# Layer 3 of three batch tiles in two column halves, and their layer 4 ahead of the next tile's layer 1

## The reference

```python
fm = emb_table[jnp.arange(N_CAT)[None, :], cat_idx]          # gather, 26 x 128 per sample
h = relu(dense_x @ Wd1 + bd1); h = relu(h @ Wd2 + bd2)
dense = relu(h @ Wdf + bdf)
Z = concatenate([fm, dense[:, None, :]], axis=1)             # 27 x 128
S = einsum('bie,bje->bij', Z, Z)
x = concatenate([S[:, iu, ju], dense], axis=-1)              # 351 + 128
x = relu(x @ Wt1 + bt1)                                      # 1024
x = relu(x @ Wt2 + bt2)                                      # 1024
x = relu(x @ Wt3 + bt3)                                      # 512
x = relu(x @ Wt4 + bt4)                                      # 256
return sigmoid(x @ Wo + bo)
```

## Time and profile before

| | |
|---|---|
| median of 3 runs | 173.36 us (173.22 to 175.69) |
| the profiled execution | 173.28 us, of which the span from first to last instruction is 171.5 us |
| instructions | 3942 |
| PE busy | 160.8 us, 94% of the span |
| PE weight loads | 115.3 us, 67% |
| DVE, ACT, POOL busy | 71.0, 67.0 and 99.2 us |
| granted TensorE clock | 1.000 over the span |

### The profile page before, as it was taken

The page is one execution under the profiler, slowest core; times in us unless marked ns, Lnnn a source line. Parts: engine busy times, 40 slices in busy tenths (PEclk is TensorE's granted clock), DMA queues, the critical chain, the costliest instruction groups (busy, mean ns, idle before and its releaser), DMA issues.

```text
span 171.5 us, 3942 instructions
## 1 busy us (share of the span) xinstructions
PE 160.8 (94%) x1703; PEld 115.3 (67%) x1703; DVE 71.0 (41%) x143; ACT 67.0 (39%) x121; POOL 99.2 (58%) x111
## 2 busy tenths in 40 slices
PE   1999998867799999999999999999999999999995
PEld 1334464423677878767877886777777777788993
DVE  4005267953657457363513045244122262322230
ACT  3368598755657767142202132411111231201202
POOL 3777777777777777777777777777777000000000
DMA  3999655665997552122212222122222000000000
GB/s 49 279 387 310 185 170 177 175 184 168 307 341 259 171 179 55 54 61 46 61 50 57 54 54 57 46 61 50 58 49 57 23 4 0 0 4 0 0 0 0
DMA packets 6674, 18.18 MB, mean 106 GB/s; under 512 B 2309, under 2 KB 2441, under 8 KB 6530
## 3 DMA queue, kind: packets, MB, share of 16 engines
q1 hardware_dynamic: 3330, 11.12, 19.8%
q0 software_dynamic: 3328, 6.82, 15.3%
HBM read 17.93 MB, written 0.00 MB: 105 GB/s over the span
## 4 chain that ended last, share of the span: by engine, by line
PE 71%; DMA 23%; ACT 3%; DVE 1%; issue 0%
PE mp L489 27%; DMA w<-in_wt 22%; PE mp L456 10%; PE mp L514 8%; PE tp L464 6%; PE gp L417 5%; PE gp L407 5%; PE gp L533 3%; PE tp L550 3%; PE gp L429 1%; DMA idx<-in_cat_idx 1%; PE mp L558 1%; ACT xb L671 1%; DVE xb L829 1%; ACT xp L673 1%; ACT w2h L636 1%
## 5 line engine op out<-in xcount | busy, mean ns | idle before, releaser
L350 POOL DMA_INDIRECT rows<-in_emb,row_of x104 | 98.3, 945 | 33.3 <-issue 29.6
L489 PE MATMUL mp<-w2l,a1h 128*128 128x512 f32 x64 | 26.8, 418 | 0.0
L489 PE MATMUL mp<-w2h,a1h 128*128 128x512 f32 x64 | 26.1, 408 | 0.0
L489 PE MATMUL mp<-w2h,a1l 128*128 128x512 f32 x64 | 25.4, 397 | 0.0
L407 PE MATMUL gp<-ident,rows 128*128 128x128 f32 x104 | 17.3, 276 | 2.6 <-DMA rows<-in_emb,row_of 2.5
L662 ACT COPY zt<-gp 128x512 f32<-128x512 f32 x16 | 9.4, 586 | 25.3 <-PE gp L407 25.1
L407 PEld LDWEIGHTS gp<-ident,rows 128*128 128x128 f32 x104 | 12.9, 140 | 9.2 <-DMA rows<-in_emb,row_of 5.0
L852 DVE TENSOR_TENSOR raw<-mp,bc 128x512 f32<-128x512 f32 x8 | 5.5, 692 | 26.1 <-PE mp L489 26.1
L417 PEld LDWEIGHTS gp<-zt 128*32 128x32 f32 x1024 | 10.9, 110 | 6.9 <-issue 6.6
L489 PEld LDWEIGHTS mp<-w2h,a1l 128*128 128x128 f32 x64 | 12.1, 189 | 2.8 <-DVE a1l L846 0.9
L803 DVE TENSOR_TENSOR w2l<-w,tp 128x1024 fp32r<-128x1024 f32 x7 | 8.5, 1220 | 12.9 <-ACT tp L647 12.9
(11 more groups left out here) (89 smaller groups left out, 247.6 us busy)
## 6 DMA issues: line engine op xcount, KB each, us to landing
w<-in_wt SPq DMA_DIRECT2D x13, 512.0 KB, 4.5
rows<-in_emb,row_of POOLq DMA_INDIRECT x104, 2.7
w<-in_wt SPq DMA_DIRECT2D x3, 468.0 KB
bc<-in_rows SPq DMA_DIRECT2D x1, 1024.0 KB
wd_sb<-in_wd SPq DMA_DIRECT2D x1, 512.0 KB, 3.6
w1d<-in_wt SPq DMA_DIRECT2D x1, 512.0 KB, 7.2
bt<-in_rows SPq DMA_DIRECT2D x1, 512.0 KB, 9.5
wdf_sb<-in_wdf SPq DMA_DIRECT2D x1, 128.0 KB, 3.1
```

What stands on the lines that cost most here:

```text
L350: pool.indirect_dma_start(out=rows[:, n % RING, :], out_offset=None, in_=emb.rearrange("c v e -> (c v) e"), in_offset=bass.IndirectOffsetO ...
L489: last = pe.matmul(sums_of(t, 2 + h), a[:, k, :], w[:, k, cols], start=(k == 0 and part == 0), stop=(k == M1 - 1 and part == 2))
```

## The change

For the tiles 0 to 2, layer 3 is done in four quarters of 12 matmuls with 256 columns each, 48 instead of 24 with 512: columns 0 to 255 for the input chunks 0 to 3, columns 256 to 511 for the same chunks, and then both for the chunks 4 to 7. The halves have a bank of mp each. DVE adds the bias for each half (layer_3_sum(t, h), 256 columns). The turn of the first half stands at n = 40 of the 48, that of the second half behind the loop; each is two transposes into tp[0], followed by a relu of 256 columns. Gram set 3 moves from inside the loop to behind it, ahead of the second turn. Layer 4 then runs ahead of the next layer 1, with the pair chunks 0 and 1 ahead of its fourth product and chunk 2 behind it. ACT does both relus ahead of pairs_out. DVE does both sums ahead of turn_sums. The positions in layer 3 of the feature groups, of gram set 2 and of the turn of layer 2 are counted in half-width matmuls and are other ones. Each tile now counts six turns instead of five. The last split of w3 goes through tp[0] instead of mp[1]. All that comes ahead of layer 3 of tile 0 keeps its order.

```diff
-FEATURES_3 = [{1: [5], 7: [6], 9: [7], 12: [8]}] * 3 + [{}]
+FEATURES_3 = [{2: [5], 24: [6], 31: [7], 40: [8]}] * 3
-GRAMS_3 = [{5: 2, 14: 3}] * 3 + [{}]
-TURN_3_IN_1, LAYER_4_IN_1 = 3, 6
+GRAMS_3 = [{14: 2}] * 3
+HALVES_3, QUARTER_3 = 2 * PRODUCTS_3, PRODUCTS_3 // 2
-FIRST_PAIRS = PRODUCTS_3 - 3
+CHUNKS_IN_4 = 3
-TURN_2B = 4
-TURNS = 5
+TURN_2B, TURN_3 = 10, 40
+TURNS = 6
...
+        def sums_of_3(t, h):
+            return mp[:, (SUMS * t + 4 + h) % 2, 0:2 * P]
...
+            if n >= SPLITS_H1:
+                return tp[:, 0, :]
...
-                    if n == TURN_3_IN_1 and t > 0:
-                        turn(t - 1, 4)
-                    if n == LAYER_4_IN_1 and t > 0:
-                        layer_4(t - 1)
...
-                for n in range(PRODUCTS_3):
-                    if t == 0 and n == 3 * SPLITS[SPLITS_H1][1]:
+                for n in range(HALVES_3):
+                    quarter, r = divmod(n, QUARTER_3)
+                    h, k, part = quarter % 2, M2 // 2 * (quarter // 2) + r // 3, r % 3
+                    if t == 0 and h == 0 and part == 0 and k == SPLITS[SPLITS_H1][1]:
                         pe.wait_ge(w_lo, len(SPLITS))
...
-                    if n == FIRST_PAIRS:
-                        transpose_pairs(t + 1, range(FIRST_CHUNKS))
...
+                    if n == TURN_3:
+                        turn_3(t, 0)
...
-                    last = pe.matmul(sums_of(t, 4), a[:, k, :], w[:, k, :], start=(n == 0), stop=(n == PRODUCTS_3 - 1))
-                last.then_inc(l3_ready, 1)
+                    last = pe.matmul(sums_of_3(t, h), a[:, k, :], w[:, k, h * 2 * P:(h + 1) * 2 * P],
+                                     start=(quarter < 2 and r == 0), stop=(quarter >= 2 and r == QUARTER_3 - 1))
+                    if quarter >= 2 and r == QUARTER_3 - 1:
+                        last.then_inc(l3_ready, 1)
+                grams(t + 1, SETS - 1)
+                turn_3(t, 1)
+
+            def turn_3(t, h):
+                pe.wait_ge(raw_ready, TURNS * t + 4 + h + 1)
+                if h == 1:
+                    pe.wait_ge(a3_ready, 2 * t + 1)
+                for c in range(2 * h, 2 * h + 2):
+                    last = pe.transpose(tp[:, 0, c * P:(c + 1) * P], raw[:, 0, c * P:(c + 1) * P], ident[:])
+                last.then_inc(turned, 1)
...
                 for k in range(M3):
-                    if k == 0:
-                        pe.wait_ge(a3_ready, t + 1)
+                    if k % 2 == 0:
+                        pe.wait_ge(a3_ready, 2 * t + k // 2 + 1)
+                    if k == CHUNKS_IN_4:
+                        transpose_pairs(t + 1, range(FIRST_CHUNKS))
...
                 layer_3(t)
+                layer_4(t)
                 transpose_pairs(t + 1, range(FIRST_CHUNKS, PAIR_CHUNKS))
...
                 if n == SPLITS_H1:
-                    sc.wait_ge(raw_ready, 4)
+                    sc.wait_ge(a2_lo, 1)
...
+                relu_3(t, 0)
+                relu_3(t, 1)
                 pairs_out(t + 1)
-                relu_3(t)
...
+                    if n == HALVES_3 - QUARTER_3:
+                        layer_3_sum(t, 0)
+                layer_3_sum(t, 1)
                 turn_sums(t + 1)
-                layer_3_sum(t)
                 pairs_lo(t + 1)
                 last_layers(t)
```

More of the change, by code:

```diff
@@ L279, in split_bank @@
         def split_bank(n):
+            if n >= SPLITS_H1:
+                return tp[:, 0, :]
             if n >= WHOLE_SPLITS:
-                return mp[:, 0 if SPLITS_H0 <= n < SPLITS_H1 else 1, :]
+                return mp[:, 0 if n >= SPLITS_H0 else 1, :]
             rows_of = PC if SPLITS[n][0] == "w1" else P
@@ L505, in layer_3 @@
                         turn(t, 3)
-                    if n == FIRST_PAIRS:
-                        transpose_pairs(t + 1, range(FIRST_CHUNKS))
[L508 to L512, removed]
-                    a, w = ((a2h, w3h), (a2h, w3l), (a2l, w3h))[part]
-                    last = pe.matmul(sums_of(t, 4), a[:, k, :], w[:, k, :], start=(n == 0), stop=(n == PRODUCTS_3 - 1))
-                last.then_inc(l3_ready, 1)
+                    if n == TURN_3:
+                        turn_3(t, 0)
+                    if h == 0 and r == 0:
+                        pe.wait_ge(a2_hi, 2 * t + quarter // 2 + 1)
+                    if h == 0 and r == 2:
+                        pe.wait_ge(a2_lo, 2 * t + quarter // 2 + 1)
+                    a, w = ((a2h, w3h), (a2h, w3l), (a2l, w3h))[part]
+                    last = pe.matmul(sums_of_3(t, h), a[:, k, :], w[:, k, h * 2 * P:(h + 1) * 2 * P],
[11 more added lines that the diff above has]
+                last.then_inc(turned, 1)
             def last_layer_3(t):
@@ L555, in last_layer_4 @@
                 for k in range(M3):
-                    pe.wait_ge(a3_ready, t + (1 if k < 2 else k))
+                    pe.wait_ge(a3_ready, 2 * t + (1 if k < 2 else k))
                     for m in range(2):
@@ L684, in layer_2_hi, with relu_3 @@
                 sc.activation(a2h[:, 4 * h:4 * h + 4, :].rearrange("p m b -> p (m b)"), tp[:, h, :], ACT.Relu).then_inc(a2_hi, 1)
-            def relu_3(t):
-                sc.wait_ge(turned, TURNS * t + 5)
-                sc.activation(a3[:].rearrange("p m b -> p (m b)"), tp[:, 0, :], ACT.Relu).then_inc(a3_ready, 1)
+            def relu_3(t, h):
+                sc.wait_ge(turned, TURNS * t + 4 + h + 1)
+                sc.activation(a3[:, 2 * h:2 * h + 2, :].rearrange("p m b -> p (m b)"), tp[:, 0, 2 * h * P:2 * (h + 1) * P], ACT.Relu).then_inc(a3_ready, 1)
             def sigmoid():
@@ L859, in layer_2_lo, with layer_3_sum @@
                                         op0=ALU.max, op1=ALU.subtract).then_inc(a2_lo, 1)
-            def layer_3_sum(t):
-                ve.wait_ge(l3_ready, t + 1)
-                ve.tensor_tensor(raw[:, 0, :], sums_of(t, 4), bc[:, ROW3:ROW3 + TOP[3]], ALU.add).then_inc(raw_ready, 1)
+            def layer_3_sum(t, h):
+                cols = slice(2 * h * P, 2 * (h + 1) * P)
+                ve.wait_ge(l3_ready, 2 * t + h + 1)
+                ve.tensor_tensor(raw[:, 0, cols], sums_of_3(t, h), bc[:, ROW3 + cols.start:ROW3 + cols.stop], ALU.add).then_inc(raw_ready, 1)
             def last_layers(t):
@@ L950, in _ @@
             for k0, k1 in ((0, 2), (2, 3), (3, 4)):
-                ve.wait_ge(l3_ready, t + k0 // 2 + 1)
+                ve.wait_ge(l3_ready, 2 * t + k0 // 2 + 1)
                 ve.tensor_tensor(raw[:, 0, k0 * P:k1 * P], gp[:, 2 + k0 // 2, (k0 % 2) * P:((k1 - 1) % 2 + 1) * P],
```

## The result

The changed kernel takes 172.38 us (median of 20 runs, 171.14 to 174.44); the kernel before takes 173.34 us (median of 20 runs beside them, 173.16 to 175.69). The ratio is 0.9938, with a 95% interval of 0.9919 to 0.9958: no change by the measure of 2%, but a gain of about 1 us where 0.3 us of loss was forecast. The profiled execution took 172.31 us.

A forecast was written before the change was run, and what follows sets the result against it. PE, busy 94% of the span, was taken to bound the kernel. Terms +0.57 - 0.21 - 0.39 + 0.55 - 0.25 = +0.27 us on the 173.36 median gave 173.6 us, range 172.3 to 174.8.

The forecast's parts named there:

- Gram set 3, the pairs and layer 4: Behind layer 3: gram set costs PE the same, pair transposes wait longer under layer 4's shorter cover; +0.55 us together.
- Halving layer 3: Layer 3, tiles 0 to 2: 48 matmuls at 0.120 us replace 24 at 0.232; +0.19 a tile, +0.57 in all.
- The turn of layer 3: First half's turn at n = 40: excess 0.14 instead of 0.21, second half's turn covered; -0.21 us in all.
- The turn of layer 1: Inside layer 1: DVE is free earlier, so the turn's wait falls from 0.14 to about 0.01; -0.39 us in all.
- The rest: Later feature groups remove tile 0's 0.17 row wait, and tile 2's 0.08 ahead of layer 4 goes: -0.25 us together.
- The pair wait goes: Rival at the pair transposes: 1.37 us of excess vanishes, giving 172.3 us; chance 0.16.
- The relu blocks the pairs: Rival on ACT: late second-half relu delays the copy of xb; 0.4 of lateness gives 174.4 us; chance 0.16.
- the interruptions: Rival in layer 3: six breaks a tile in the half-width stream cost 0.08 more each, +1.5, 175.1 us; chance 0.05.
- It does nothing: Rival: turn waits stay, pairs stay hidden, only the halves' +0.57 counts: 173.9 us, inside the likeliest case (0.60).
- The claim that 2.33 us is all there is: Excess at the three layer 3 to layer 1 boundaries totals 2.33 us, all that a better order could win.

The follow-up runs named there:

- after_early: The changed kernel with feature groups 6, 7, 8 of layer 3 back at their earlier places (n = 14, 18, 24): 173.56 us, ratio 1.0045.
- early_free: The changed kernel with feature groups 6, 7, 8 at n = 14, 18, 24 and four gathers of tile 0 left out: 174.52 us, ratio 1.0041.
- before_free: The kernel before with four of tile 0's 26 gathers left out, zeros in their slots: 173.72 us, ratio 0.9949.
- before_again: The kernel before, unchanged, profiled once more: 174.55 us, ratio 1.0018.
- after_again: The changed kernel, unchanged, profiled once more: 173.12 us, ratio 0.9960.
- after_quick: The changed kernel with ACT's last cast of the fill moved behind the pick of the pairs: 172.54 us, ratio 0.9962.
- after_quick_2: A repeat of the changed kernel with ACT's last cast of the fill moved behind the pick of the pairs: 172.39 us, ratio 0.9934.
- after_split: The changed kernel with the matmul ahead of each gram set of layer 2 issued as two of 256 columns: 172.49 us, ratio 0.9951.
- before_quick_2: A repeat of the kernel before with ACT's last cast of the fill moved behind the pick of the pairs: 173.27 us, ratio 0.9973.
- before_quick: The kernel before with ACT's last cast of the fill moved behind the pick of the pairs: 173.40 us, ratio 0.9968.
- after_free: The changed kernel with four of tile 0's 26 gathers left out: 174.54 us, ratio 1.0008.
- before_held: The kernel before with PE held ahead of layer 1 of tile 0 until gathered rows of tile 1's g1 arrive: 179.58 us, ratio 1.0410.
- after_held: The changed kernel with PE held ahead of layer 1 of tile 0 until gathered rows of tile 1's g1 arrive: 181.02 us, ratio 1.0441.
- before_fewer: The kernel before without one of its 104 gathers (category 8 of tile 1): 173.26 us, ratio 0.9991.
- halves_alone: The kernel before with all but the first and last matmul of layer 3 issued as two of 256 columns: 174.08 us, ratio 1.0022.

## Why the prediction was wrong

It held that the three stretches would gain 0.30 by their excess, lose 0.57 by the halves, and that nothing else moved. The sign came out wrong, and the step that failed is "Gram set 3, the pairs and layer 4". It said that the gram set costs PE the same wherever it stands, and that the pairs would then wait 0.40 and cost 0.55 more. The set's edges became 0.39 cheaper over three tiles, the pairs waited 0.17, and their cost didn't rise.

Excess summed over the three tiles of the two first profiles is 3.90 before and 2.30 after. The table goes through the same intervals between matmuls at the prices of the prediction (the halves' row has in it what the plain intervals of layer 3 were cheaper than 0.120):

| step | predicted | measured |
|---|---|---|
| halves | +0.57 | +0.39 |
| turn of layer 3, first half | -0.21 | -0.14 |
| turn of layer 1 | -0.39 | -0.34 |
| edges of gram set 3, with the second half's turn behind it | 0 | -0.39 |
| pairs and layer 4 | +0.55 | -0.03 |
| rows, relu of tile 2 | -0.25 | -0.48 |
| length of gram sets | 0 | +0.52 |
| sum | +0.27 | -0.47 |

The stretches themselves differ by -0.51; 0.04 is small gaps that I don't place.

**Halving layer 3** was right in mechanism, and a little dear in size: 105.90 - 105.78 = 0.12 a matmul, and the median over layer 3 of tiles 0 to 2 is 0.118, not the 0.120 of the last tile. The Trainium skill (TensorE: Matmul & The Clock Gate, Back-to-back issue gap) gives 81 ns at 128 columns and 131 ns at 512. By the estimate from these two in the prediction the halves would have cost 4.7. The traces don't agree: 118 ns at 256 columns and 232 ns at 512.

**The turn of layer 3** was right in mechanism and size: PE arrives at 104.60 + 0.11, goes at 104.80 (0.09 of wait, 0.08 said), and pays about 0.06 for the restart: 0.15 for 0.14. after_early and early_free show what it hangs on: without g8's transpose in front (g8 at n = 24 there) the wait is 0.20. The second half's turn, said to cost nothing, doesn't wait, but costs the 0.05 behind the gram set.

**The turn of layer 1** was right: 0.08 is left of 0.20 (112.85 to 113.84 in tile 1, less 0.464 and 0.44), and 0.08 was said.

**Gram set 3, the pairs and layer 4** is the step that failed, in its first sentence, that the gram set costs PE the same wherever it is. It had an edge of 0.17 to 0.18 ahead, of which 0.08 was a wait for g8's copy, and 0.11 behind; now 0.09 and 0.05: 3 x 0.13 = 0.39. The rows for it stood in the earlier trace rows (104.17) and the page, but I only priced the work between gram set and pairs. The chain behind was right in tile 1 to the hundredth (g + 2.66) where the set took 0.92; but there PE came later by the same 0.23, at g + 2.49, so the wait was 0.17, not 0.40. In tiles 0 and 2 the short case held (g + 2.43), against an arrival at g + 2.26 as predicted: 0.17 again. I had counted a long DVE start (g + 1.02) behind a short gram set. Before, the two do go together in tiles 0 and 1 of the profiles of the old order, but not in tile 1 of before_free and of before_again (set of 0.72, DVE at g + 0.83). After, in 14 of the 15 sets 3 of after, after_again, after_quick, after_quick_2 and after_split, DVE starts 0.07 to 0.12 behind the set's end, short or long: the chain is late only when PE is late too. The fifteenth, tile 0 of after_again, is the forecast case, with its wait of 0.43. The relu didn't hold ACT's copy of xb: in tile 1 the copy (107.79) starts before the relu's 0.38 are over (107.88).

**The rest** was too small. The relu wait of tile 2 cost 0.31 before with its restart, not the 0.08 of the chain. The rows cost 0.17 in the first profile and 0.79 in before_quick_2: not a fixed term but a floor at 75.2, which goes with POOL's steady issues (two profiles and the times above are what shows it). The later places of g6 to g8 take the kernel off it. I had argued this only for the one wait that I saw.

**The rivals.** "The pair wait goes" (172.3, 0.16) names the number (172.38 was measured) and half the mechanism: DVE's start was mostly the short one. That the number fits is luck, since 0.17 of wait a tile stayed, and half of the gain lies outside the three stretches. "The relu blocks the pairs" and the interruptions did not happen. "It does nothing" neither.

**The claim that 2.33 us is all there is** left out the edges (3 x 0.28 at gram set 3 alone), the floor, and all outside the three stretches. There the first pair of profiles differs by 0.23 ahead of layer 3 and 0.26 in layer 2 (gram sets of 0.90 and 0.73 before, 0.68 after), half of the 1.0 us.

How far this explains the 0.96 us. Six pairs of profiles can be compared in the three stretches, with their six gram sets taken out:

| pair | stretches, old and new form | six gram sets | the rest |
|---|---|---|---|
| before, after | 51.37, 50.86 | 4.24, 4.76 | -1.03 |
| before_again, after_again | 51.44, 51.34 | 4.66, 5.01 | -0.46 |
| before_quick, after_quick | 51.08, 50.88 | 4.08, 4.81 | -0.93 |
| before_quick_2, after_quick_2 | 52.04, 50.45 | 4.21, 4.32 | -1.71, of which 0.79 is the floor |
| before_free, after_free | 51.31, 50.27 | 4.54, 4.15 | -0.65 |
| before_held, after_held | 51.07, 51.14 | 4.08, 4.98 | -0.83 |

So the new form's program is shorter in every pair, by 0.5 to 1.0 us without the floor, and longer gram sets take 0.1 to 0.9 of it back in five of the six. These are not shown to be luck: in the seven profiles of each form (these, before_fewer and after_split) 16 of 42 sets took 0.84 or more in the new form and 5 of 42 in the old one. They may be a price of the new form. The whole times of the four pairs with all gathers and no hold differ by 0.96, 1.43, 0.86 and 0.88 us in their medians, and by 1.1, 1.0, 0.1 and 0.7 by their ratios. That the gain comes from the stretches and the floor is likely, not shown to the tenth; in the first pair of profiles half of it lies outside the stretches.

What stays open:

- Why the fill's last weight load came earlier in the first pair, and whether the change has a part in it. ACT takes it (w2h) at 42.07 to 43.44 in five profiles of kernels with the old order and at 40.39 to 41.90 in nine with the new, though the diff moves no load. But the held pair, whose hold stands behind that load, has it the other way round: 41.13 in before_held and 42.07 in after_held. Most of the first pair's 0.98 is given back in layer 2 of tile 0, where rows are late.
- What makes a gram set take 0.68 or 0.91, and why the long ones are more frequent in the new form. It isn't the neighbours alone: set 3 of tile 1 took 0.92 in after and 0.68 in after_quick_2, with the same ones.
- Why DVE starts at g + 1.0 behind a short set in the old form, and now and then in tile 0 or 1 of the changed form (after_again in tile 0, and with early features after_early in tile 1 and early_free in tile 0, where the pairs wait 0.43, 0.44 and 0.40 for 0.17). It never does in tile 2, behind POOL's last gather (132.4), and no gram set 3 of the changed form was long there either. That points to the gathers; no run takes them away.

## What to carry to other kernels

When a block of small matmuls is moved, price its edges as well as its length: what the stream paid between the last matmul ahead and its first, and what stood two instructions ahead that it reads. A wait hidden in an edge (here 0.08 for a copy) has no row of its own; compare the gap with the same gap elsewhere. And where a steady queue feeds the bound engine, look for the floor it sets, by making the engine arrive earlier, before pricing its wait from one profile.

## What the runs showed of the hardware

- The same 64 small matmuls take mostly 0.67 to 0.69 us or 0.87 to 0.92 (some lie between), and the DVE operation that follows gram set 3 starts mostly at g + 0.80 or g + 1.03: both by steps of about 0.23.
- From the end of a DVE copy to the weight load of the gram set that waits for it: 0.11 to 0.12 us in six places, and the matmul 0.03 to 0.04 behind.
- A product of type fp32r with its own weight load takes 0.232 us at 512 columns and 0.118 at 256 in the middle of a stream, at a granted clock of 1.00.
- In before_again, halves_alone and early_free the granted clock fell to the lower of its two levels (1.2 of 2.4 GHz) as layer 1 of tile 0 began (its mean from 44 to 52 us is 0.79), and that layer took 6.98 us instead of 5.38. PE had been idle for 1.9 to 2.7 us in one piece shortly before. An idle piece of 2.85 us in before_free was not followed by a fall.
- Row blocks land 2.4 us after issue at the least and 2.9 in the median, but up to 6.5 (changed kernel).
